# A two-branch transformer block on one core: how and when the slot map of its expert layer is built

## The reference

```python
xn = _layernorm(x, axis=-1)
x = x + attn(xn) + ffn(xn)
# attn: 16 heads, each with two q/k pairs of 8 columns; o = a1 - lam * a2, rms norm, projection
# ffn: 8 experts, top 2, capacity C = 2 * T // 8 = 1024
logits = tokens @ wg
idx1 = argmax(softmax(logits)); idx2 = argmax(logits without idx1)
loc1 = cumsum(mask1) - mask1; loc2 = cumsum(mask2) - mask2 + sum(mask1)
keep = loc < C;  f = idx * C + minimum(loc, C - 1)          # slot of each token, one per choice
disp[f] += tokens * keep
h = gelu(einsum('ecd,edf->ecf', disp, w_gate)); eo = einsum('ecf,efd->ecd', h, w_down)
out = g1 * keep1 * eo[f1] + g2 * keep2 * eo[f2]
```

## Time and profile before

| | |
|---|---|
| three runs, median (lowest, highest) | 1813.76 us (1813.74, 2590.47) |
| the profiled execution: its own time | 1814.34 us |
| its span, first to last instruction | 1812.5 us |
| TensorE clock granted, mean | 0.991 |
| busy: PE / DVE / ACT / POOL | 1719.5 (95%) / 1487.0 (82%) / 1403.3 (77%) / 578.5 (32%) us |
| the chain that ended last | PE 78%, ACT 15%, POOL 3%, DVE 2% |
| of it, POOL L557 | 2% |

### The profile page before, as it was taken

How to read it: one execution, slowest core, us unless ns; L and a number is a source line. 1 busy time by engine, 2 the same in 40 slices (tenths; PEclk the granted TensorE clock), 3 DMA queues, 4 the chain that set the end, 5 groups by cost and what they waited for, 6 DMA issues and landing times.

```text
span 1812.5 us, 39337 instructions
## 1 busy us (share of the span) xinstructions
PE 1719.5 (95%) x15555; PEld 748.2 (41%) x15555; DVE 1487.0 (82%) x1727; ACT 1403.3 (77%) x2639; POOL 578.5 (32%) x1065
## 2 busy tenths in 40 slices
PE   6869999999999999999999999999999999999898
PEld 5437888888885222222222222222222222222226
DVE  7767777777767999998999989899999999999913
ACT  4535455445435999999999989999999999999993
POOL 1474221222100345455454554542121211112230
PEclk9989999999999999999999999999999999999999
DMA  7564232212203111111111111110101011100002
GB/s 238 198 223 138 93 111 91 67 63 91 85 24 106 40 39 43 41 34 44 40 44 41 34 40 44 41 38 22 31 24 30 25 28 27 27 11 5 5 1 94
DMA packets 92281, 109.66 MB, mean 61 GB/s; under 512 B 17473, under 2 KB 67265, under 8 KB 92097
## 3 DMA queue, kind: packets, MB, share of 16 engines
q1 hardware_dynamic: 85952, 90.36, 15.9%
q0 software_dynamic: 6144, 16.79, 3.2%
HBM read 72.77 MB, written 33.82 MB: 59 GB/s over the span
## 4 chain that ended last, share of the span: by engine, by line
PE 78%; ACT 15%; POOL 3%; DVE 2%; issue 1%; DMA 1%; SPq 0%; ACTq 0%; DVEq 0%; POOLq 0%
PE banks L1222 25%; PE banks L1210 15%; ACT arena_t L779 13%; PE banks L1261 10%; PE banks L1241 10%; PE banks L1192 10%; POOL arena_v L557 2%; PE banks L1281 2%; ACT o_raw L758 2%; PE banks L1115 2%; PE banks L1343 2%; PE banks L1161 1%; PE banks L1126 0%; DMA arena_x<-x_in 0%; PE banks L1334 0%
## 5 line engine op out<-in xcount | busy, mean ns | idle before, releaser
L992 DVE TENSOR_REDUCE row_half<-banks 128x2 f32<-128x1024 f32 x1024 | 1189.3, 1217 | 153.7 <-PE banks L1192 149.8
L779 ACT ACTIVATE arena_t<-banks 128x512 f32<-128x512 f32 x2048 | 1085.4, 599 | 59.8 <-PE banks L1210 34.0
L1222 PE MATMUL banks<-arena_t,v_ring 128*17 128x256 f32 x8192 | 643.5, 386 | 37.3 <-ACT o_raw L758 37.2
L1222 PEld LDWEIGHTS banks<-arena_t,v_ring 128*17 128x17 f32 x8192 | 136.2, 95 | 416.7 <-issue 241.4
L1210 PE MATMUL banks<-arena_q 50*128 50x512 bf16 x960 | 286.3, 384 | 0.6 <-ACT arena_t L779 0.6
L1210 PE MATMUL banks<-qk_ring 50*128 50x512 bf16 x896 | 266.2, 386 | 5.2 <-DVE arena_r L1040 2.5
L1192 PE MATMUL banks<-arena_q 48*128 48x512 bf16 x960 | 269.6, 384 | 0.0
L1192 PE MATMUL banks<-qk_ring 48*128 48x512 bf16 x896 | 251.1, 384 | 2.9 <-DVE row_half L992 1.4
L743 ACT ACTIVATE arena_t<-banks 128x512 f32<-128x512 f32 x128 | 76.5, 598 | 206.0 <-PE banks L1241 197.3
L1261 PE MATMUL banks<-w_parts,hidden_parts 128*128 128x256 f32 x1536 | 196.3, 286 | 0.0
L1261 PEld LDWEIGHTS banks<-w_parts,hidden_parts 128*128 128x128 f32 x1536 | 187.1, 192 | 13.5 <-issue 13.4
(11 more groups left out here) (147 smaller groups left out, 1356.6 us busy)
## 6 DMA issues: line engine op xcount, KB each, us to landing
expert_rows<-arena_r SPq DMA_DIRECT2D x16, 512.0 KB, 3.0
q_stack<-arena_q SPq DMA_DIRECT2D x8, 768.0 KB, 4.7
k_stack<-arena_q SPq DMA_DIRECT2D x8, 768.0 KB, 3.4
v_heads<-arena_v SPq DMA_DIRECT2D x4, 1088.0 KB, 5.6
v_ring<-v_heads SPq DMA_DIRECT2D x64, 68.0 KB, 2.9
arena_x<-x_in SPq DMA_DIRECT2D x4, 1024.0 KB, 6.3
token_rows<-arena_x SPq DMA_DIRECT2D x4, 1024.0 KB, 7.8
arena_v<-w_gate_in SPq DMA_DIRECT2D x4, 1024.0 KB, 6.2
```

Of the source, the lines that this page charges most:

```text
L779: nc.scalar.activation(probs[:, kt % PSLOTS, q, :], banks[:, ST_BANKS[ring_place(i) % 3], :], ACT.Exp).then_inc(exp_done, 1)
L992: nc.vector.tensor_reduce(halves[:, :, j // 2], banks[:, SMAX_PAIRS[m % 2]:SMAX_PAIRS[m % 2] + 2, :], AX.X, ALU.max, negate=True).then_inc ...
L1222: mm = pe.matmul(banks[QUAD * q:QUAD * q + VP, OT_BANK, columns], v_ring[:, g % SLOTS, kt, :], probs[:, kt % PSLOTS, q, columns], start=(k ...
```

## The change

Everything in it lies in stage 2 and at its two ends.

- Layout. The one-hot sides are turned: the 64 (choice, tile) columns now stand innermost, `[P, n, 64]`. A constant `numbers` (8192 bf16, value n repeated 64 times) is made by one POOL `iota` at the start, in the space of the first gate weights. Slots are kept in bf16 (`low_bf`, `tile_bf`).
- DVE makes both sides alone: 8 `tensor_tensor` of 128x2048 and one `tensor_scalar` of 128x4096, behind the rests of units 2 to 6. All operands are bf16, except the per-partition scalar `lane`. POOL's 40 instructions go.
- PE makes the map after unit 7, with `low_side[:, :, k]` as weights and `tile_side[:, :, :, k]` as moving data; neighbouring elements of both lie 64 elements (128 bytes) apart, where they were adjacent. `find_tokens` stands after `split_low(7)`.
- PE's q/k units use three bank pairs (2, 4, 0 in turn), so unit n waits for `split_rest(n - 3)`. The last `middle`, `split_low` and store (unit 15) move behind the second gelu of the first expert step; PE waits for the last rest before its first `smax` there.
- The first gate weights are loaded behind unit 6 instead of before unit 0, the down weights behind unit 9 instead of 11. ACT rounds both (behind units 9 and 12), DVE subtracts both (behind units 10 and 13); POOL does neither.
- ACT loads the gelu table right after its exponentials in unit 0, with a dummy activation, and the exp table after the last expert step.

```diff
-COUNT_AT, MAP_AT, ROWS_AT = 1, 11, 14
+COUNT_AT, MAP_AT, ROWS_AT = 1, 7, 14
+SIDES = 9
+HIGH_AT, LOW_AT = (9, 12), (10, 13)
-LOW_BY_POOL = NT + GROUP
...
-        low_side = arena_v[:, 2 * W_PART:4 * W_PART].bitcast(BF16).rearrange("p (c t n) -> p c t n", c=2, t=NT)
-        tile_side = arena_r[:, 4 * CH:12 * CH].bitcast(BF16).rearrange("p (c t i n) -> p c t i n", c=2, t=NT, i=2)
+        numbers = arena_v[:, 0:2 * W_PART].bitcast(BF16).rearrange("p (n k) -> p n k", n=P)
+        low_side = arena_v[:, 2 * W_PART:4 * W_PART].bitcast(BF16).rearrange("p (n k) -> p n k", n=P)
+        tile_side = arena_r[:, 4 * CH:12 * CH].bitcast(BF16).rearrange("p (i n k) -> p i n k", i=2, n=TILES)
...
-        FIRST_ROWS_BANK, ROWS_BANK = 4, 2
+        FIRST_ROWS_BANK, ROWS_BANK = 6, 2
...
+        def qk_bank(n):
+            return 2 * ((n + 1) % 3)
...
-            load_gate(0, 0)
...
-                    if n == 11:
+                    if n == 6:
+                        sp.wait_ge(sides_ready, SIDES)
+                        load_gate(0, 0)
+                    if n == 9:
                         sp.wait_ge(map_psum, 1)
                         load_down(0, 0)
...
-            nc.gpsimd.iota(in_tile[:], pattern=[[1, P]], base=0, channel_multiplier=0,
+            nc.gpsimd.iota(numbers, pattern=[[1, P], [0, 2 * NT]], base=0, channel_multiplier=0,
...
-            for i in range(LOW_BY_POOL):
-                c, t = divmod(i, NT)
-                low = nc.gpsimd.tensor_scalar(low_side[:, c, t, :], in_tile[:], slot_low[:, c, t:t + 1], None, ALU.is_equal)
-            low.then_inc(low_side_ready, 1)
-            first_weights_low(0)
             pool.wait_ge(xn_out, 16 * B)
             pool.wait_ge(map_ready, 1)
             for n in range(2):
                 find_rows(n)
-            pool.wait_ge(down_in[0], 16)
-            nc.gpsimd.tensor_copy(w_parts[0][:, 1, HI], w_ring[0][:, 1, LO]).then_inc(first_high, 1)
-            first_weights_low(1)
...
+            for n in range(4 * B):
+                part1(n)
                 if n == ROWS_AT:
                     rows_t_high(0)
+                if n + 1 < 4 * B:
+                    middle(n)
                 if n == 0:
...
+                    load_table(ACT.Gelu)
-                if n == 4:
-                    act.wait_ge(gate_in[0], 16)
-                    nc.scalar.copy(w_parts[0][:, 0, HI], w_ring[0][:, 0, LO]).then_inc(first_high, 1)
+                if n == HIGH_AT[0]:
+                    first_weights_high(0, gate_in)
+                if n == HIGH_AT[1]:
+                    first_weights_high(1, down_in)
...
+                    if n == 0 and f == 1:
+                        middle(4 * B - 1)
...
+            load_table(ACT.Exp)
...
+            def tile_is(h):
+                rows = slice(h * HALF_S, (h + 1) * HALF_S)
+                nc.vector.tensor_tensor(tile_side[:, 1, rows, :], numbers[:, rows.start + 1:rows.stop + 1, :], over(tile_bf, HALF_S),
+                                        ALU.is_equal).then_inc(sides_ready, 1)
...
+            def tile_lanes():
+                dve.wait_ge(sides_ready, 4)
+                nc.vector.tensor_scalar(tile_side[:, 1], tile_side[:, 1], lane[:, 0:1], None, ALU.mult).then_inc(sides_ready, 1)
+
+            def low_is(q):
+                rows = slice(q * QUARTER, (q + 1) * QUARTER)
+                nc.vector.tensor_tensor(low_side[:, rows, :], numbers[:, rows, :], over(low_bf, QUARTER),
+                                        ALU.is_equal).then_inc(sides_ready, 1)
...
+            def first_weights_low(which):
+                dve.wait_ge(first_high, which + 1)
+                nc.vector.tensor_tensor(w_parts[0][:, which, LO], w_ring[0][:, which, LO], w_parts[0][:, which, HI].bitcast(F32),
+                                        ALU.subtract).then_inc(first_low, 1)
...
+                if n == COUNT_AT + 1:
+                    tile_is(0)
+                if n == COUNT_AT + 2:
+                    tile_is(1)
+                    tile_tokens(0)
+                if n == COUNT_AT + 3:
+                    tile_tokens(1)
+                    tile_lanes()
+                if n in (COUNT_AT + 4, COUNT_AT + 5):
...
+                    for q in range(2):
+                        low_is(2 * (n - COUNT_AT - 4) + q)
                 if n == ROWS_AT:
                     rows_t_low(0)
-                split_low(n)
+                if n + 1 < 4 * B:
+                    split_low(n)
+                if n == MAP_AT:
+                    find_tokens()
+                if n in LOW_AT:
+                    first_weights_low(LOW_AT.index(n))
...
+                    if n == 0 and f == 1:
+                        split_low(4 * B - 1)
...
+                for k in range(2 * NT):
+                    mm = pe.matmul(banks[:, MAP_BANK, 0:2 * TILES], low_side[:, :, k], tile_side[:, :, :, k].rearrange("p i n -> p (i n)"),
+                                   start=(k == 0), stop=(k == 2 * NT - 1))
...
+                if n >= 3:
+                    pe.wait_ge(rest_ready, n - 2)
...
+                        mm = pe.matmul(banks[:, qk_bank(n) + half, :], w_qk[:, c, m * P:(m + 1) * P],
...
+                    if n == 0 and f == 1:
+                        pe.wait_ge(rest_ready, 4 * B)
```

More of the change, by code:

```diff
@@ L545, in find_rows @@
                         in_offset=bass.IndirectOffsetOnAxis(ap=token_i[:, 4 * n + t:4 * n + t + 1], axis=0)).then_inc(rows_in_s[s], 16)
[L547 to L550, removed]
-            for s in range(2):
-                pool.wait_ge(v_out[s], 32)
-            pool.wait_ge(slots_ready, 1)
-            for i in range(LOW_BY_POOL):
-                c, t = divmod(i, NT)
-                low = nc.gpsimd.tensor_scalar(low_side[:, c, t, :], in_tile[:], slot_low[:, c, t:t + 1], None, ALU.is_equal)
-            low.then_inc(low_side_ready, 1)
-            first_weights_low(0)
             pool.wait_ge(xn_out, 16 * B)
@@ L711, in rows_t_high, with part1 @@
                     nc.scalar.copy(rows_parts[:, HI, c, :], banks[:, rows_bank(n) + c, :]).then_inc(rows_high, 1)
-            for n in range(4 * B):
+            def part1(n):
                 s = n % PARTS
@@ L880, in split_rest @@
                 dve.wait_ge(part1_ready, n + 1)
-                nc.vector.scalar_tensor_tensor(out=rest[:, s, :], in0=banks[:, 2 * s:2 * s + 2, :].rearrange("p a n -> p (a n)"),
+                nc.vector.scalar_tensor_tensor(out=rest[:, s, :], in0=banks[:, qk_bank(n):qk_bank(n) + 2, :].rearrange("p a n -> p (a n)"),
                                                scalar=SCALE if n % 4 < 2 else 1.0, in1=parts[:, n % PARTS, 0, :],
@@ L908, in find_slots @@
+                link(nc.vector.scalar_tensor_tensor(out=tile_bf[:], in0=slot_tile[:], scalar=1.0, in1=keep[:],
                                                     op0=ALU.add, op1=ALU.mult))
-            HALF_T = NT // 2
-            def low_is(t):
-                tiles = slice(t, t + GROUP)
-                nc.vector.tensor_tensor(low_side[:, 1, tiles, :], in_tile[:].unsqueeze(1).broadcast_to([P, GROUP, P]),
-                                        slot_low[:, 1, tiles].unsqueeze(2).broadcast_to([P, GROUP, P]), ALU.is_equal).then_inc(low_side_ready, 1)
@@ new lines, in tile_tokens @@
+            def tile_tokens(h):
+                rows = slice(h * HALF_S, (h + 1) * HALF_S)
+                dve.wait_ge(sides_ready, h + 1)
+                nc.vector.tensor_tensor(tile_side[:, 0, rows, :], tile_side[:, 1, rows, :], over(first_token, HALF_S),
+                                        ALU.mult).then_inc(sides_ready, 1)
+            def tile_lanes():
+                dve.wait_ge(sides_ready, 4)
+                nc.vector.tensor_scalar(tile_side[:, 1], tile_side[:, 1], lane[:, 0:1], None, ALU.mult).then_inc(sides_ready, 1)
@@ L1145, in map_slots @@
             def map_slots():
-                pe.wait_ge(low_side_ready, 4)
-                pe.wait_ge(tile_side_ready, 4)
-                for c in range(2):
-                    for t in range(NT):
-                        mm = pe.matmul(banks[:, MAP_BANK, 0:2 * TILES], low_side[:, c, t, :], tile_side[:, c, t].rearrange("p i n -> p (i n)"),
-                                       start=(c == 0 and t == 0), stop=(c == 1 and t == NT - 1))
+                pe.wait_ge(sides_ready, SIDES)
+                for k in range(2 * NT):
+                    mm = pe.matmul(banks[:, MAP_BANK, 0:2 * TILES], low_side[:, :, k], tile_side[:, :, :, k].rearrange("p i n -> p (i n)"),
+                                   start=(k == 0), stop=(k == 2 * NT - 1))
                 mm.then_inc(map_psum, 1)
```

77 lines of the change are left out of this document (26 added, 51 removed).

## The result

The median went from 1814.14 to 1820.04 us (the kernel before was run again beside it, hence not 1813.76): a ratio of 1.0035, 95% interval 1.0024 to 1.0046. I had forecast 5.3 us less, and it became 5.9 more, outside my range. One of the five runs of before took 2590.47 us and does not count in the ratio. The profiled execution has a span of 1819.9 us, 7.4 more than before.

The account below looks back on a forecast made before the run. SP's DMA queue was taken to pace the q/k stage; the third gate product (f = 2) moves from 148.3 to 142.1, less 0.9 for late weights: 5.3 us gained, 1808.4 us; twenty per cent may lie outside 1803.0 to 1815.5.

Parts of the forecast that it names:

- Start of SP's queue: Unit 4's store in the q/k stage: issued at 85.7, 3.7 us later, from ACT's table load and more DVE work.
- DVE gets no gain from 16 bits: Rival on DVE's map sides: eight instructions at 2.28 us each, about 8 us later, total 1816; chance 8%.
- The map's start: PE's map after unit 7: starts at 94.4, when DVE has finished the last of the nine sides.
- The map's length: PE's 64 map matmuls read at 128 bytes: 7.5 us, between 5.3 and 18.3, costing 1.8 us.
- The turning point of about 12.8 us: Map length in the q/k stage from which the change was said to turn from gain to loss.
- the strided map is dear: Rival on PE's map: 10.6 us gives 1811.5, 18.3 gives 1819.2; 27% for over 9.5 us, a third beyond 12.8.
- Unit 8: Q/k unit behind the map: PE about 3.5 us, ready 8.3 us after the map.
- SP's pace behind unit 8: SP's DMA queue in the q/k stage: 5.07 us per unit, down weights issued behind unit 9 at 118.6.
- POOL's rows hidden behind SP: Q/k stage before the change: SP sets the pace from 82 to 124 us, hiding POOL's row up to 112.
- Landing of the down weights: First expert's down weights: land 7.0 us after issue, at 125.6, with ACT waiting behind unit 12.
- The chain behind them: From the down weights' landing through ACT, DVE and PE to the third gate product (f = 2): 14.7 us.
- Late stall: First expert step: next expert's gate weights slip behind unit 15's later store, costing 0.9 us (0 to 3).

Follow-up runs that it names:

- w = 2: The changed kernel with the 64 map columns in groups of two, so PE reads at 4 bytes instead of 128; ratio 0.9986 to the kernel before.
- the kernel with everything together: Changed kernel with groups of two, row loads of heads 1 to 3 behind the second expert's weights, unit 15 in place; ratio 0.9950 to before.

## Where the prediction was right and where it failed

- **Start of SP's queue: right.** Unit 4's store at 85.38 (said 85.7); VectorE's 2048 in bf16 takes 1.216 us (1.25), the 4096 1.29 (1.4). "DVE gets no gain from 16 bits" is out.
- **The map's start: right,** 93.35 (94.4).
- **The map's length: the step that failed.** "I take 7.5, in the lower part, since the elements are still 16-bit" and "only the distance changes". It was 16.34, and 8.84 of the 12.35 us by which f = 2 came too late are this term. What was wrong in it: a stride of 128 bytes on the moving operand alone takes the map from 5.36 to 14.12 us, so the distance, which I had at 2.2 us, is the whole price, and 16 bits do not soften it. The upper bound, 18.3, held, but by luck: it came from the f32 matmul of 128x256, which says nothing about a stride. The turning point of about 12.8 us is not refuted: the sign turns somewhere between a map of 7.72 us (0.9984) and one of 14.12 (1.0018). The 27% for "the strided map is dear" was the case that came, in its far third.
- **Unit 8: 1.6 us too little,** because I costed PE's part at full clock behind the map; the granted clock was 0.50 up to 113, and PE took 5.20 us, not 3.5.
- **SP's pace behind unit 8: right,** 119.57 to 129.53 for two units is 9.96 (10.14 said). The runs with the loads moved show it as a cause, not only as a coincidence.
- **POOL's rows hidden behind SP: half right.** In the kernel before, with SP's loads moved away, POOL's rows still end at 112.5 and f = 2 comes only 1.6 us earlier. The two chains were about equally long there.
- **Landing of the down weights:** 7.42 in the change (7.0). With a quick map and SP's loads in place it was 10.2 to 10.8 in the five kernels that have them (10.27 with w = 2, ACT waiting), so with the map at 5.3 I would have been 3.3 us off here. With a slow map it was 6.7 to 7.4, and with the loads moved 7.7 and 8.2. That points at row loads still under way, but it was not isolated.
- **The chain behind them: 2.8 us too short** (14.7 said; 136.97 to 154.45 is 17.5). I let f = 2 follow the rest of unit 15, but PE starts its first gate product only when the first rows' low part is written, and has 12 matmuls and a pair of maxima before f = 2. (In the kernel before, the 12 matmuls ran beside the end of unit 15, out of the chain.) That took 6.17 us (148.28 to 154.45) at a granted clock of 0.50, where I had 3.05. In the kernel with everything together it is 4.91 us, with the clock at 0.50 at first and 1.00 from 138 on.
- **Late stall: right in kind,** 1.48 (0.9, bound 3). ACT waited 3.05 us for the next gate weights.
- **Iota 7.58 us on POOL, hidden: right.**

Summed for f = 2, forecast 142.1: map start -1.05, map +8.84, unit 8 up to its store +1.58, SP -0.18, landing +0.42, chain +2.8, together +12.4; measured 154.45, +12.35.

With a map of 5.36 us (w = 2) f = 2 came at 146.0 instead of the 140.3 that I would have said: issue 0.4, landing 3.3, chain 2.0. So also without the failed step the gain would have been 2.4 us (1794.06 against 1796.46), not 7.1. The mechanism of the sum held, then, but two of its terms, landing and chain, were too small as well.

## What to carry to other kernels

A layout that gives one engine its fast mode is paid by whoever reads it: before the innermost dimension is turned, look at the stride at which PE's moving operand will be read, and keep neighbours within 4 bytes if both sides can have it (groups of two did: VectorE kept 1.22 us for 2048 elements, and PE's map took 5.36 us as with adjacent reads). When the bound of a stage is taken away, work out the next one in the same sum (here SP's loads) and change both, or the gain stays small. And if an unseen price has bounds on both sides of the sign, give the dear half the chance that the bounds give it; that the elements are still 16-bit was no evidence about distance.

## What the runs showed of the hardware that I had not expected

- The map's moving operand (128 columns, 16-bit) costs 84 ns a matmul at 4 bytes between elements, 121 at 8, 237 at 16, 255 at 128 (both operands strided); strided weights alone 99 (6.34 / 64), a strided moving operand alone 221 (14.12 / 64). The figures below 125 are means over both clocks. At 1.00 alone, in 97 to 99, 2 us hold 36 matmuls at 4 bytes, 20 at 8 bytes, and 25 with strided weights alone; at 0.50 they hold 22 at 4 bytes and 10 at 16 and at 128.
- At 8 bytes the granted clock makes no difference to that pace (20 matmuls in 2 us at 0.54 and at 1.00). At 16 and at 128 bytes the clock stayed at 0.50 through 15 and 16 us of matmuls without a gap, where at 4 and at 8 bytes it stood at 1.00 from 97 on, in a map that had started at 93.7.
- VectorE's `tensor_tensor` in bf16 keeps 1.22 us for 2048 elements when its inner run is only two elements long.
